# Stores issued by GpSimd on its own queue instead of by SyncE

## The reference

```
x = x + einsum('bct,bcd->bdt', x, weights[itok_B_0_15])       # 128x128 matrix of the batch's condition
Bx  = einsum('bni,bri->bnr', x, B[itok_B_4_50])               # rank 16, over the 2048 time steps
out = einsum('bnr,bor->bno', Bx, A[itok_B_4_50]) * 1.0
x = x + out
```

## Time and profile before

| quantity | value |
| --- | --- |
| median of three runs | 401.35 us |
| the profiled execution | 401.69 us |
| its span (first to last instruction) | 399.8 us |
| TensorE matmul busy | 379.0 us (95%) |
| VectorE busy | 271.3 us (68%) |
| ScalarE busy | 221.7 us (55%) |
| GpSimd busy | 29.8 us (7%) |
| bytes moved | 152.37 MB, mean 381 GB/s |
| stores issued | 62 of 1 MB, 8 of 256 KB, all by SyncE |

### The profile page before, as it was taken

One profiled execution on the slowest core, in us unless ns is written; L12 is line 12 of the kernel. 1 busy time (PEld: TensorE's weight loads), 2 busy tenths in 40 slices (PEclk: granted clock), 3 DMA queues, 4 the chain that ended last, 5 costly groups with the idle time before them and its releaser, 6 DMA issues.

```text
span 399.8 us, 16408 instructions
## 1 busy us (share of the span) xinstructions
PE 379.0 (95%) x6144; PEld 349.7 (87%) x6144; DVE 271.3 (68%) x576; ACT 221.7 (55%) x513; POOL 29.8 (7%) x71
## 2 busy tenths in 40 slices
PE   1999999999999999999999999999999999999962
PEld 1899999999999999999999999999999999999951
DVE  0067677668667767766866776776686677678684
ACT  1465565566556556556555655555555565565540
POOL 1110000000000000000000000000000000000000
PEclk9999999999999999999999999999999999999995
DMA  7999999999999999999999999999999999999546
GB/s 224 331 421 380 403 391 409 390 418 395 406 402 393 404 399 415 396 402 407 398 398 403 415 381 407 402 405 403 404 406 394 409 403 397 404 403 371 233 185 236
DMA packets 29777, 152.37 MB, mean 381 GB/s; under 512 B 3268, under 2 KB 3524, under 8 KB 13764
## 3 DMA queue, kind: packets, MB, share of 16 engines
q1 hardware_dynamic: 29764, 152.19, 96.6%
HBM read 85.07 MB, written 67.11 MB: 381 GB/s over the span
## 4 chain that ended last, share of the span: by engine, by line
PE 91%; DMA 3%; DVE 2%; SPq 2%; issue 1%; DVEq 0%; ACT 0%
PE f_bank L314 58%; PE low_bank L344 17%; PE z_bank L328 15%; DMA x_in<-in_x 3%; DVE x_out L247 2%; SPq L127 0%; DVE z_pair L273 0%; SPq L130 0%; SPq L135 0%; SPq L115 0%; SPq L131 0%; SPq L121 0%; DVE z_all L278 0%; DVE at L265 0%; DVEq L49 0%
## 5 line engine op out<-in xcount | busy, mean ns | idle before, releaser
L314 PE MATMUL f_bank<-m_sel,x_in 128*128 128x128 f32 x2048 | 247.7, 280 | 9.4 <-POOL m_sel L183 8.4
L314 PEld LDWEIGHTS f_bank<-m_sel,x_in 128*128 128x128 f32 x2048 | 235.6, 193 | 17.1 <-issue 9.3
L205 ACT COPY ft<-f_bank 128x512 f32<-128x512 f32 x256 | 149.8, 586 | 81.8 <-PE f_bank L314 80.7
L247 DVE TENSOR_TENSOR x_out<-low_bank,ft 128x512 f32<-128x512 f32 x256 | 158.9, 682 | 4.3 <-PE low_bank L344 2.4
L273 DVE TENSOR_TENSOR z_pair<-z_bank,z_two 16x128 f32<-16x128 f32 x128 | 36.8, 287 | 105.2 <-ACT z_two L213 103.1
L344 PE MATMUL low_bank<-z_all,at 16*128 16x128 f32 x2048 | 76.0, 285 | 5.3 <-DVE x_out L247 5.3
L344 PEld LDWEIGHTS low_bank<-z_all,at 16*128 16x128 f32 x2048 | 63.8, 188 | 18.8 <-issue 18.8
L328 PE MATMUL z_bank<-ft,ab_in 128*16 128x128 f32 x2048 | 68.3, 274 | 0.0
L221 ACT COPY z_all<-z_all 16x128 f32<-16x128 f32 x128 | 37.8, 296 | 51.1 <-DVE z_all L278 49.5
L328 PEld LDWEIGHTS z_bank<-ft,ab_in 128*16 128x16 f32 x2048 | 50.3, 96 | 7.8 <-issue 0.2
L177 POOL TENSOR_TENSOR m_sel<-w_all,ident 128x128 f32<-128x128 f32 x62 | 28.1, 454 | 317.4 <-PE f_bank L314 285.1
(11 more groups left out here) (1 smaller groups left out, 0.0 us busy)
## 6 DMA issues: line engine op xcount, KB each, us to landing
x_in<-in_x SPq DMA_DIRECT2D x63, 1024.0 KB, 9.2
out<-x_out SPq DMA_DIRECT2D x62, 1024.0 KB, 7.2
ab_in<-in_lora SPq DMA_DIRECT2D x64, 256.0 KB, 8.0
out<-x_out SPq DMA_DIRECT2D x8, 256.0 KB, 2.9
x_in<-in_x SPq DMA_DIRECT2D x4, 256.0 KB, 4.1
w_first<-in_L_cond_weights SPq DMA_DIRECT2D x2, 64.0 KB, 5.0
ids<-in_itok_B SPq DMA_DIRECT2D x2, 0.2 KB
w_all<-in_L_cond_weights SPq DMA_DIRECT2D x1, 0.5 KB, 9.0
```

The source lines that it names most:

```text
L205: nc.scalar.copy(ft[k][u][:], f_bank[BANK_OF[u]][:]).then_inc(copied, 1)
L247: nc.vector.tensor_tensor(x_out[k][:, UNIT * u:UNIT * (u + 1)], low_bank[u][:], ft[k][u][:], ALU.add).then_inc(added, 1)
L314: last = nc.tensor.matmul(f_bank[BANK_OF[u]][:, P * c:P * (c + 1)], x_in[k][:, UNIT * u + P * c:UNIT * u + P * (c + 1)], m_sel[k][:], star ...
```

## The change

GpSimd gets the store of batch b-2 at the end of its step b, behind `pick_m`, with the same wait on `added`; it also gets the eight quarter stores and the last waits. SyncE keeps the loads. Sizes, buffers, semaphores and their values stay as they are.

```
 sync:
                         load_ab((k - 1) % BODY, adapter)
-                    if begun(b - 2):
-                        sp.wait_ge(added, UNITS * (b - 1))
-                        sp.dma_start(out[b - 2], x_out[(k - 2) % BODY][:]).then_inc(stored[(k - 2) % BODY], 16)
...
-            for b in (BATCHES - 2, BATCHES - 1):
-                for u in range(UNITS):
-                    cols = slice(UNIT * u, UNIT * (u + 1))
-                    sp.wait_ge(added, UNITS * b + u + 1)
-                    sp.dma_start(out[b, :, cols], x_out[b % BODY][:, cols]).then_inc(stored[b % BODY], 16)
-            for k in range(BODY):
-                sp.wait_ge(stored[k], 16 * (TURNS if k < BODY - 2 else TURNS - 1 + UNITS))
 gpsimd:
                         pick_m((k + 3) % BODY, b + 3)
+                    if begun(b - 2):
+                        pool.wait_ge(added, UNITS * (b - 1))
+                        nc.gpsimd.dma_start(out[b - 2], x_out[(k - 2) % BODY][:]).then_inc(stored[(k - 2) % BODY], 16)
...
+            for b in (BATCHES - 2, BATCHES - 1):
+                for u in range(UNITS):
+                    cols = slice(UNIT * u, UNIT * (u + 1))
+                    pool.wait_ge(added, UNITS * b + u + 1)
+                    nc.gpsimd.dma_start(out[b, :, cols], x_out[b % BODY][:, cols]).then_inc(stored[b % BODY], 16)
+            for k in range(BODY):
+                pool.wait_ge(stored[k], 16 * (TURNS if k < BODY - 2 else TURNS - 1 + UNITS))
```

## The result

The changed kernel takes 408.63 us (median of 4 runs, 408.56 to 409.0), beside 401.59 us for the kernel before in 4 runs. The ratio is 1.0177, with a 95% interval from 1.0159 to 1.0195: 7.0 us slower. The forecast was 403.0 us, in a range from 401.2 to 407.0.

What follows compares the result with a forecast made beforehand. The prediction took TensorE to bound the kernel from 20.12 us, with the stores as the path at the end. It added 0 (start), 0 (62 periods) and 1.63 us (end) to 401.35, giving 403.0 us, range 401.2 to 407.0.

Steps and rivals of the forecast that it cites:

- What bounds the kernel: From 20.12 us on TensorE alone, 5.87 us a batch; no transfer sets any of the 62 periods.
- rival B: In the steady part, interleaved loads and stores fall below 402 GB/s and DMA becomes the bound: 411.8 us at 380; chance 0.10.
- SyncE's side: In each period SyncE loses a wait and a 0.36 us issue; loads leave up to 0.91 us earlier, gain 0.
- The pick behind a store: In the periods GpSimd's pick waits behind a store, done at 159.8 us, needed at 172.7: 12.9 us spare, cost 0.
- The store's landing: In the periods a store lands 7.2 us after issue, with 13.7 us of cover before VectorE rewrites its buffer: cost 0.
- The price of an issue: On GpSimd, 0.88 us for each store's issue, taken from that of `w_all`, and once 0.23 us between instructions.
- The end: Last four quarter stores, issued every 0.88 us, finish at 398.28 us in place of 396.65: +1.63 us, landing unchanged at 2.6.
- C: GpSimd's issues take 2 us or more, hidden in the steady part; the end grows 6.1 us to 407.5 us; chance 0.06.
- signs of being wrong: TensorE's part stretching, the first 20 us stretching, or the 1.9 us around the span growing would show the forecast wrong.

Runs made afterwards that it cites:

- e6: The kernel before, with all stores and the last waits moved from SyncE to ScalarE, a second hardware queue: 402.27 us, ratio 1.0000.
- e1: The changed kernel, with the eight quarter stores and the last waits back on SyncE and 62 stores still on GpSimd: 401.92 us, ratio 1.0007.
- e9: The changed kernel with one more GpSimd drain in the last turn, behind the store of batch 59: 403.57 us, ratio 1.0043 to the kernel before.
- e3: The kernel before, with only the very last quarter store issued by GpSimd, which waits for its landing: 401.6 us, ratio 1.0004.
- e10: The changed kernel with a GpSimd drain at the end of each of its 64 steps, behind every 1 MB store: 519.02 us, ratio 1.2863.
- e7: The changed kernel with each of the 62 stores split by time steps into halves of 128 rows, 132 DMAs in all: 407.47 us, ratio 1.0131.
- e8: The changed kernel with each of the 62 stores split into halves of 64 rows of 8 KB, 132 DMAs in all: 406.05 us, ratio 1.0110.

## Why the prediction was wrong, point by point

- **What bounds the kernel** was read rightly. The periods are unchanged to 0.01 us, and rival B (two queues move less than one) was wrong: 402 GB/s and no wait for a transfer in the middle. The waits of 1.1 and 0.8 us on a load end at 20.50 us, where the first mixing of the chain begins. So did those of 0.5 and 0.2 us before, at 20.12: the prediction counted them into the 362 us, but they are the end of the start. e6 has two queues at ratio 1.0000.
- **SyncE's side, gain 0**: right. The load now leaves at 153.65 us, 0.2 us after the mixing that it waits for, and lands in 9.2 us as before.
- **The pick behind a store, cost 0**: right. The pick that the prediction followed, forecast to be done at 159.8 us, runs from 160.16 to 160.60, right behind the store at 159.30, and TensorE never waits for `m_sel` in the periods.
- **The store's landing**: it takes 9.4 in place of 7.2 us. I had left that unchanged; 13.7 us of cover take it, as e1 shows.
- **The price of an issue**: mis-sized, 0.54 us and 0.06 between two in place of 0.88. That is just the pace of the additions, so the queue of issues that made up my 1.63 us doesn't form. In its place stand the 0.48 us of a later start and end of the last issue, and 0.4 us of a longer landing, which I had left out: 0.9 us. So this part of the forecast, 1.63 us, was too big by 0.7.
- **The step that failed** is "The end". It closed with "The landing after that (2.6 us) I leave as it is", and took the end of the landing for the end of the kernel. Behind it GpSimd's closing drain was missing: 5.79 us with 70 software DMAs behind it, 5.7 us of the difference. Without it the changed kernel would take 408.6 - 5.7 = 402.9 us; e9, which keeps 0.9 us of drain, has 403.57.
- **The rivals**: none had it. C named 407.5 us, which is near, but by luck: it rests on slow issues, and these are faster than forecast. Its own sum is also short, as four issues of 2 us from 389.68 would run to 397.68 and past the 394.53 from which it counts, so that the last would end at 405.9 and the time be 410.6 us. Of the signs of being wrong that the prediction named, none told of this: TensorE's part did not stretch, the start moved by 0.38 us, and 1.7 us lie around the span in place of 1.9. Could the trace of before have told? Not the size: its only row is a drain of 0.55 us with no software DMA before it. But that row shows that the drain exists and that it is hidden only because GpSimd has finished 40 us early; the change makes GpSimd the last engine to finish. What I asked of each moved instruction I should have asked of the instruction behind the last one.

No version tried beats the kernel before: e1, e3 and e6 equal it (ratios 1.0007, 1.0004 and 1.0000), and there was little to win: TensorE waits for no store in it, and the issue of the last store takes 0.33 us.

## What to carry to other kernels

When work moves to another engine, see which engine finishes last now, and what it still has to do behind its last instruction; the page doesn't count sequencer instructions as busy, so an idle end is to be looked up by line. DMAs issued by GpSimd cost about 0.08 us each at its next drain (up to 70 of them here), whatever their size: have another engine issue the last few and wait for them, so that GpSimd drains early (e1). Don't put a drain between a store and work that needn't wait for its landing (e10). A queue of its own for the stores brought nothing here (e1, e6), where no load on the path waited behind a store.

## What the runs showed of the hardware that was not expected

The drain's price itself: 0.082 us per software DMA, for 256 KB, 128 KB and 1 MB alike, and 0.09 for 256 bytes. ScalarE's drain behind 70 stores took 0.008 us. Where a store was still under way, GpSimd's drain outlasted its landing, by 0.07 us with one DMA to clear and by 2.9 with 70. After more than a hundred DMAs an issue pauses (2.66 us in e7; in e8 the DMA went 3.2 us after its addition was done).

VectorE's one operation with two SBUF inputs grew longer when the later pick fell onto it, in e7 with a mean of 342 ns in place of 280; in the changed kernel itself the mean stayed at 280. The timeline of e7 shows the two together:

```profile
358.44 0.45 POOL L167 TENSOR_TENSOR m_sel<-w_all,ident 128x128 f32<-128x128 f32 x1 [0.66 <-issue]
358.46 0.88 DVE L281 TENSOR_TENSOR z_all<-z_pair 16x128 f32<-16x128 f32 x2
```

Two of them take 0.88 us here, 0.59 undisturbed. The Trainium skill (SBUF — State Buffer, section Who interferes with whom) says that a VectorE instruction with two SBUF inputs contends with a GpSimd one that reads SBUF; the trace agrees. It cost nothing there: in e8, where the mean is 320 ns, TensorE waits for nothing between 21 and 382 us.
